# A gated two-layer block on one Trainium2 core: routing from unscaled rows, late work between expert steps, zeroing in two parts, GpSimd's clears between batches

## What is computed

```python
x = x + tanh(g_xattn[0]) * _L0_xattn_ref(ctx_512, _layernorm(x), ...)
x = x + tanh(g_ffn[0]) * _L0_ffn_ref(_layernorm(x), gate_w, w13, w2)
x = x + tanh(g_xattn[1]) * _L1_xattn_ref(_layernorm(x), ctx_512, ...)
x = x + tanh(g_ffn[1]) * _L1_ffn_ref(_layernorm(x), ...)

# _L0_xattn_ref: sim = Q K^T; each row keeps its 76 largest entries, sigmoid, made symmetric
# _L0_ffn_ref, NUM_EXPERTS = 64, TOP_K = 8:
logits = x @ gate_w.T
probs = softmax(logits); topk_w, topk_idx = top_k(probs, 8)
for e in range(64):
    h = silu(x @ w13_e[:128].T) * (x @ w13_e[128:].T)
    out += combine[:, e] * (h @ w2_e.T)
```

## Time and profile before

| | us |
|---|---|
| median of 3 runs | 563.62 |
| lowest and highest | 560.38, 567.36 |
| profiled execution, own time | 561.23 |
| its span in the profile | 559.3 |
| last scatter of a batch's rows starts | 137.56 |
| first matmul of the expert steps | 142.85 |

### The profile page before, as it was taken

One profiled execution on the slowest core, in us unless ns is written; L12 is line 12 of the kernel. 1 busy time (PEld: TensorE's weight loads), 2 busy tenths in 40 slices (PEclk: granted clock), 3 DMA queues, 4 the chain that ended last, 5 costly groups with the idle time before them and its releaser, 6 DMA issues.

```text
span 559.3 us, 9235 instructions
## 1 busy us (share of the span) xinstructions
PE 412.9 (74%) x2738; PEld 347.8 (62%) x2738; DVE 344.4 (62%) x1053; ACT 184.5 (33%) x377; POOL 148.6 (27%) x156
## 2 busy tenths in 40 slices
PE   5345642500799999999823676799789988998796
PEld 3234441400798888988622554797678867996695
DVE  4988876279334444443346893488667885680664
ACT  3122220100233333343236143524453354427321
POOL 4017775757000000000477723330424000000000
PEclk9999999755699999999965879799999999999999
DMA  7999222237599999999832201110212000000000
GB/s 238 424 416 403 91 94 76 94 112 282 146 293 303 324 317 313 331 355 385 279 98 75 86 22 56 39 39 2 59 39 75 2 0 0 20 1 2 2 19 20
DMA packets 36789, 82.96 MB, mean 148 GB/s; under 512 B 6032, under 2 KB 16144, under 8 KB 34960
## 3 DMA queue, kind: packets, MB, share of 16 engines
q1 hardware_dynamic: 23616, 56.48, 29.2%
q0 software_dynamic: 6144, 16.79, 9.4%
q10 hardware_dynamic: 6992, 9.24, 4.6%
HBM read 50.44 MB, written 31.92 MB: 147 GB/s over the span
## 4 chain that ended last, share of the span: by engine, by line
PE 50%; DVE 13%; issue 12%; POOL 7%; ACT 7%; SPq 4%; DMA 3%; another core or an unknown queue 2%; ACTq 1%; DVEq 0%; POOLq 0%
PE PS L606 9%; POOL slots_in L447 7%; PE PS L616 6%; PE PS L695 5%; PE PS L772 3%; PE PS L708 3%; PE PS L709 3%; PE PS L710 3%; PE PS L593 2%; PE PS L669 2%; DMA XE<-slots_in 2%; PE PS L790 2%; PE PS L800 2%; PE PS L757 2%
## 5 line engine op out<-in xcount | busy, mean ns | idle before, releaser
L454 POOL DMA_INDIRECT GB<-slots_out,IDXG x64 | 70.2, 1096 | 221.1 <-DMA slots_out<-OE 133.3
L606 PE MATMUL PS<-XTE,WR 128*128 128x128 f32 (+2 forms) x512 | 80.5, 301 | 0.0
L447 POOL DMA_INDIRECT slots_in<-XNA,IDX x64 | 64.9, 1014 | 38.3 <-issue 30.8
L606 PEld LDWEIGHTS PS<-XTE,WR 128*128 128x128 f32 x512 | 71.2, 195 | 0.3
L1302 DVE TENSOR_TENSOR HE<-SGE,PS 128x128 f32<-128x128 f32 (+2 forms) x64 | 19.9, 312 | 71.7 <-ACT SGE L927 66.3
L616 PE MATMUL PS<-WR,HE 128*80 128x256 f32 (+2 forms) x198 | 53.3, 380 | 0.5 <-issue 0.5
L918 ACT COPY XTE<-PS 128x256 f32<-128x256 f32 (+2 forms) x64 | 26.3, 410 | 73.1 <-PE PS L593 72.0
L708 PE MATMUL PS<-XH,WGH 128*128 128x256 f32 x160 | 50.3, 314 | 0.0
L593 PE MATMUL PS<-CF,XE 80*128 80x80 f32 (+2 forms) x198 | 28.6, 258 | 26.2 <-DMA XE<-slots_in 26.0
L695 PE MATMUL PS<-WD,XW 128*128 128x256 f32 x160 | 42.6, 389 | 5.8 <-DVE TH L1391 5.8
L593 PEld LDWEIGHTS PS<-CF,XE 80*128 80x128 f32 (+2 forms) x198 | 22.9, 145 | 36.5 <-DMA XE<-slots_in 29.7
(11 more groups left out here) (226 smaller groups left out, 814.9 us busy)
## 6 DMA issues: line engine op xcount, KB each, us to landing
WR<-in_wexp SPq DMA_DIRECT2D x64, 384.0 KB
slots_in<-GB SPq DMA_DIRECT2D x12, 1024.0 KB, 18.5
XE<-slots_in SPq DMA_DIRECT2D x24, 160.0 KB, 4.4
slots_out<-OE ACTq DMA_DIRECT2D x24, 160.0 KB
XE<-slots_in SPq DMA_DIRECT2D x29, 128.0 KB, 4.3
slots_out<-OE ACTq DMA_DIRECT2D x24, 128.0 KB
WGU<-in_wgu SPq DMA_DIRECT2D x1, 2560.0 KB
XE<-slots_in SPq DMA_DIRECT2D x11, 192.0 KB, 4.1
```

What stands on the lines that cost most here:

```text
L447: pool.indirect_dma_start(out=xs, out_offset=bass.IndirectOffsetOnAxis(ap=IDX[:, t, j:j + 1], axis=0), in_=XNA[:, t, :], in_offset=None, b ...
L454: pool.indirect_dma_start(out=GB[:, t % BT, j, :], out_offset=None, in_=ys[0:rows, :], in_offset=bass.IndirectOffsetOnAxis(ap=IDXG[:, t, j ...
L606: last = mm(psGE[place % 2][:, a, 0:cap(place)], W13[:, k, a, :], XTE[:, place % 2, k, 0:cap(place)], start=(k == 0), stop=(k == KC - 1))
```

## The change

Seven edits, in words; the diff below has the core of each.

1. Routing uses X1 itself. TensorE transposes X1, and the logits come from X1 times a gate whose column means over D were taken out (centre_gate: two products into psN, two additions on VectorE). The row's scale no longer changes which 8 are largest; it enters in the exponential (scale=RSN, a bias from the new `bias_ready`). XNA is still written, for the scatters.
2. mix adds both BASE products ahead of the wait for `masked`.
3. ranks uses MSUM, the sum of earlier masks, in place of one product per earlier tile. In the last batch the two counts are formed ahead of the ranks, and `counted` is gone.
4. The top rounds are shared out by FIRST_ROUNDS and LATER_ROUNDS.
5. The zeroing is 8 copies of the lower 128 slots of the experts (`zeroed_low`) and then 4 of the upper 64 (`zeroed`). GpSimd waits for the first before tile 0 and for the second before tile 1. norm_scale stands behind 12 scatters. The clears stand at the start of batches 1, 2 and 3, the copy of CTB with the last.
6. VectorE's work behind ORD is cut into pieces, set between its expert steps at places 1 to 12 and 29 to 34 (35 only ends it).
7. SP loads AHEAD = 3 weights before it waits for the scatters, and 5 behind.

ScalarE's scores and base of b + 2 now stand ahead of the exponential of b. The general path makes its own transposes of XNA.

```diff
+ROOT_BEHIND = 12
+LOW = 128
+AHEAD = 3
+FIRST_ROUNDS = (1, 2, 2, 3)
+LATER_ROUNDS = (3, 4, 4, 5)
...
-            for i in range(SLOTS // (8 * P)):
-                sp.dma_start(xs[i * 8 * P:(i + 1) * 8 * P, :].rearrange("(p r) d -> p (r d)", p=P), ZERO)\
-                  .then_inc(S["zeroed"], 16)
+            by_expert = xs.rearrange("(e c) d -> e c d", c=CAP)
+            for first, rows, signal in ((0, LOW, "zeroed_low"), (LOW, CAP - LOW, "zeroed")):
+                experts = P * 8 // rows
+                for e in range(0, E0, experts):
+                    part = by_expert[e:e + experts, first:first + rows, :].rearrange("e (q r) d -> q e (r d)" if rows > experts else "e (q r) d -> e q (r d)", r=8)
+                    sp.dma_start(part, ZERO).then_inc(S[signal], 16)
...
-            for e in range(RING):
-                load_slots(e, first[e])
+            for e in range(AHEAD):
+                load_slots(e, first[e])
+            for e in range(AHEAD, RING):
+                n = expert(e)
+                load_slots(e, n)
+                load_weights(e, n)
...
+            def set_between(b):
+                if b == 1:
+                    nc.gpsimd.memset(VA[:, :, :, :], 0.0).then_inc(S["pool_set"], 1)
+                    nc.gpsimd.memset(G14[:, :, :], 1.0e30).then_inc(S["pool_set"], 1)
+                    nc.gpsimd.memset(TP[:, :, :], 1.0e30).then_inc(S["pool_set"], 1)
+                elif b == 2:
+                    nc.gpsimd.memset(MOE[:, :, :], 0.0).then_inc(S["pool_set"], 1)
+                elif b == 3:
+                    pool.wait_ge(S["pool_set"], 4)
+                    nc.gpsimd.memset(VA[:, :, :, HD:HD + 1], 1.0).then_inc(S["pool_set"], 1)
+                    nc.gpsimd.tensor_copy(CTB[:, :], CT[:, 0:N]).then_inc(S["e_ctx"], 1)
...
-            pool.wait_ge(S["zeroed"], 16 * (SLOTS // (8 * P)))
+            pool.wait_ge(S["zeroed_low"], 16 * (E0 * LOW // (8 * P)))
             for t in range(TT):
+                if t == 1:
+                    pool.wait_ge(S["zeroed"], 16 * (E0 * (CAP - LOW) // (8 * P)))
+                if t % BT == 0:
+                    set_between(t // BT)
                 pool.wait_ge(S["xn_ready"], t // BT + 1)
                 pool.wait_ge(S["idx_ready"], t // BT + 1)
                 for j in range(TOP0):
-                    if t % BT == BT - 1 and j == POW_AT and t // BT + 1 < B:
-                        norm_scale(t // BT + 1)
+                    b = t // BT + 1
+                    if b < B and t % BT * TOP0 + j == ROOT_BEHIND:
+                        norm_scale(b)
...
+            def centre_gate():
+                pe.wait_ge(S["half_set"], 3)
+                for k in range(KC):
+                    last = mm(psN, MINUS_MEAN[:, :], GATE0[:, k, :], start=(k == 0), stop=(k == KC - 1))
+                last.then_inc(S["gate_summed"], 1)
+
             def logits(b):
-                pe.wait_ge(S["xn_ready"], b + 1)
+                pe.wait_ge(S["x1_kept"], b + 1)
...
-                        last = nc.tensor.transpose(psX[:, k, t * P:(t + 1) * P], XNA[:, b * BT + t, k * P:(k + 1) * P], ident)
+                        last = nc.tensor.transpose(psX[:, k, t * P:(t + 1) * P], X1[:, b * BT + t, k * P:(k + 1) * P], ident)
...
+                if b == B - 1:
+                    parts = [MSUM[:, :]] + own
+                    for i, part in enumerate(parts):
+                        mm(psN, onesb, part, start=(i == 0), stop=(i == BT))
+                    for i, part in enumerate(parts):
+                        mm(psC, part, onesb[:, 0:1], start=(i == 0), stop=(i == BT))
+                for t in range(BT):
+                    earlier = ([MSUM[:, :]] if b else []) + own[0:t]
...
+            def between(place):
+
+                early = (count_rows, set_flag, output_keys, output_rows, token_weights, split_weights)
...
                 if place:
                     copy_out(turn, place - 1)
+                if isinstance(turn, int):
+                    between(place)
```

More of the change, by code:

```diff
@@ L573, in _ @@
                     scores(b + 2)
-            for n in range(TT):
-                last = mm(psN, onesb, MB[:, n, :], start=(n == 0), stop=(n == TT - 1))
-            for n in range(TT):
-                last = mm(psC, MB[:, n, :], onesb[:, 0:1], start=(n == 0), stop=(n == TT - 1))
-            last.then_inc(S["counted"], 1)
             pe.wait_ge(S["order_set"], 1)
@@ L631, in all_tokens @@
             def all_tokens():
+                for b in range(B):
+                    pe.wait_ge(S["xnt_copied"], B + b)
+                    for k in range(KC):
+                        for t in range(BT):
+                            last = nc.tensor.transpose(psX[:, k, t * P:(t + 1) * P], XNA[:, b * BT + t, k * P:(k + 1) * P], ident)
+                    last.then_inc(S["xn_flipped"], 1)
+                pe.wait_ge(S["xnt_copied"], 2 * B)
                 with pe.Fori(0, E0 // 2) as i:
@@ L910, in _ @@
                     base(b + 2)
+                act.wait_ge(S["bias_ready"], b + 1)
+                act.wait_ge(S["rs_ready"], b + 1)
+                for t in range(BT):
+                    n = b * BT + t
+                    last = A.activation(C0[:, n, :], psL[:, t, :], ACT.Exp, scale=RSN[:, n, 0:1], bias=SM[:, n, 0:1], accum_out=SM[:, n, 1:2])
+                last.then_inc(S["exp_done"], 1)
             A.preload_act_table(ACT.Silu)
@@ L945, in all_tokens @@
                         act.wait_ge(gathered[t][j], 16)
+                for b in range(B):
+                    act.wait_ge(S["xn_flipped"], B + b + 1)
+                    A.copy(XNT[:, :, b * N:(b + 1) * N], psX).then_inc(S["xnt_copied"], 1)
                 with act.Fori(0, E0) as e:
@@ L1173, in choose @@
                 st.wait()
-                st.done(V.tensor_scalar(SM[:, b * BT:(b + 1) * BT, 0:1], L8[:, :, 0:1], -1.0, None, ALU.mult))
                 for t in range(BT):
@@ new lines, in output_keys, with output_rows @@
+            def output_keys():
+                st.wait()
+                st.done(V.tensor_scalar(FM[:, 2:3], FM[:, 1:2], SKIP, -1.0, ALU.mult, ALU.add))
+                st.done(V.tensor_tensor(KEY2[:, :, :], KEY[:, :, :], ROW[:, 1:2, :].to_broadcast([P, TT, E0]), ALU.add))
+                st.wait()
+                st.done(V.tensor_tensor(KEY2[:, :, :], KEY2[:, :, :], MB[:, :, :], ALU.mult))
+            def output_rows():
+                st.wait()
+                for t in range(TT):
+                    st.done(V.max(K8[:, t, :], KEY2[:, t, :]))
+                st.wait()
+                st.done(V.tensor_scalar(IDXG[:, :, :], K8[:, :, :], FM[:, 2:3], None, ALU.add))
@@ L1280, in _, with row_matches @@
+            def row_matches(t):
                 st.wait()
```

176 lines of the change are left out of this document (102 added, 74 removed).

## The result

| | before | after |
|---|---|---|
| median of the runs, us | 565.49 (4 runs) | 570.65 (3 runs, 568.94 to 571.42) |
| ratio, with 95% interval | | 1.0107 (1.0063 to 1.0150) |
| profiled execution, own time, us | 561.23 | 568.94 |

The changed kernel is 1.1% slower, by less than the 2% that separates "slower" from "same". I had predicted 555.0 us, 1.5% faster; 570.65 lies outside the range of 549 to 563. The three executions of the kernel after are its fast ones: a fourth took 1034.32 us and is left out as slow.

The account below looks back on a forecast made before the run. The end of GpSimd's scatters in routing was taken as the bound. With the stall they end at 132.0 us, 6.5 earlier than 138.53: 561.2 - 6.5 = 554.7, leaned up to 555 us, range 549 to 563.

Parts of the forecast that it names:

- Part 4: Zeroing: high copies led by 8 use 8 engines, so GpSimd stalls 3.0 to 5.4 us, taken 4.1, before its ninth scatter.
- Part 2: GpSimd's routing queue: clears add up to 3.7 us; without a stall batch 3 starts at 107.6 us, fewer rank products saving 0 to 1.5.
- Part 1: Routing from unscaled rows: the first scatter starts at 38.2 us instead of 43.22.
- Part 3: Last batch's scatters: 1.28 us each, 20.2 us against 22.2; 0.7 comes back if weight loads caused the slow ones.
- Part 5: Expert steps: VectorE's moved pieces cost 0, up to 1 us; three weights ahead cost 0, or 6 us if loads limit.
- A: Zeroing: no stall, high copies run on all engines, scatters end at 127.8 us, total 550.5 us; chance 0.24.
- C: Ninth scatter waits much longer for the high zeroes, with four engines a 22.4 us stall, total 573 us; chance 0.07.
- B: Expert stage eats the early gain through late weight loads (6 us) or VectorE's pieces delaying HE, total 561 us; chance 0.12.
- D: Clears and late ranks starve GpSimd's queue 2 to 3 us more, total 557 us; counted within the main case's 0.57.

Follow-up runs that it names:

- z1: Changed kernel with GpSimd's power (norm_scale) behind 10 scatters instead of 12, high zero copies still led by 8: 559.12 us, ratio 1.0024.
- x3: Kernel before with only the zeroing in two parts (high copies led by 8) and GpSimd's two waits: 566.4 us, ratio 1.0049.
- w1: Kernel before with norm_scale behind 12 scatters of a batch instead of 10: 566.58 us, ratio 1.0179.
- v1: Changed kernel with only the high zero copies led by 16 instead of 8, power behind 12 scatters: 548.43 us, ratio 0.9851.
- z4: Changed kernel with high zero copies led by 16, power behind 10 scatters, eight weights loaded ahead instead of three: 550.61 us, ratio 0.9895.
- w3: Changed kernel with high zero copies led by 16, power behind 10, clears as before the change, eight weights ahead: 548.01 us, ratio 0.9824.
- z2: Changed kernel with high zero copies led by 16, power behind 10 scatters, clears as before the change: 548.64 us, ratio 0.9855.
- Set 4: Four runs sharing one chip, w1, z2 again, w3 and w4, each against the kernel before: ratios 1.0179, 0.9850, 0.9824 and 0.9867.
- w4: Changed kernel with high zero copies led by 16, power behind 12, plus a GpSimd wait for the next batch's logits: 548.2 us, ratio 0.9867.
- x1: Changed kernel with only the high zero copies led by 16, the same kernel as v1 on another chip: 561.7 us, ratio 0.9969.

## Why the prediction was wrong

**The step that failed is Part 4's size of the stall**, "3.0 to 5.4 us of stall, I take 4.1". The mechanism was right, with its place, its 8 engines and its engine count in packets. The measured stall is 11.61 us (9.23 in z1, on another chip). Against the predicted clock of the queue:

| | predicted, us | after, us | late by |
|---|---|---|---|
| first scatter | 38.2 | 37.35 | -0.9 |
| ninth | 52.5 | 59.18 | 6.7 |
| batch 1 starts | 65.0 | 72.11 | 7.1 |
| batch 2 | 88.3 | 99.75 | 11.5 |
| batch 3 | 111.8 | 124.78 | 13.0 |
| last scatter ends | 132.0 | 144.95 | 13.0 |

The missed stall is the first 7 us. Of it, 2 are already there when the low copies end, beside the slower issuing: the eighth was issued at 17.1 us and landed 16.9 us later, at 34.0 instead of 31.8. At 213 GB/s the four high ones would then be done at 34.0 + 19.7 = 53.7; the ninth scatter starts 5.5 us behind that. These lie, as I read it, in the time shared with eight scatters and with what SP had queued behind. I had put half of the scatters' bytes at the copies' rate there, up to 2.4 us, and taken 1.1. x3 points the same way: its scatters begin five us later, and the copies land 3 us earlier. How the sharing goes in detail wasn't tried.

Part 4's two bounds came from a sum of bytes. What I left out, and what the 5.5 us suggest without proving it, is that a copy on half of the engines loses twice: the other half can't help it, and packets of others on its half delay it. The Trainium skill, DMA: Bandwidth & Descriptors, section on why a DMA increments its semaphore by 16 and not by 1, gave the number of engines, and the 32 missing packets agree with it.

**The other 6 us** arise at batches 2 and 3. Batch 2 adds 4.4 us and batch 3 1.5: GpSimd waited 4.57 and 3.32 us for IDX, where the forecast had 0 and 1.3. In front of these waits stand the choice's 5.95 us at batch 2 and KEY's 4.53 at batch 3. This is the second step that failed: Part 2 had no term for a late signal at batch 2, and at batch 3 it put down the 3.25 us from mask to KEY to the ranks' products, "worth 0 to 1.5". The row said "remote" in brackets, and 1.14 us is what KEY waits where signals are prompt (w1, v1). I read a wait without a releaser as work.

From the last scatter on, the profile of after has 1.7 us less up to the last HE and 3.0 us more behind it than the profile before. So 13.0 of the 14.2 us by which that execution missed its forecast (568.94 against 554.7) are there when the scatters end.

**Point by point.** Part 1 held: 37.35 us against 38.2, and 5.9 us earlier than before. Part 2's queue held where nothing disturbed it: v1 starts its batches at 61.55, 85.44 and 107.28 us and ends at 127.43, predicted for no stall 60.9, 84.2, 107.6 and 127.8. What it lacked was a term for the late IDX. Part 3 held: 124.78 to 143.97 us is 15 steps of 1.28, and w1, which has the old order on VectorE, still needs 1.42 (119.59 to 140.86). The doubt that it left, whether the traffic of the eight weight loads made the slow steps, is settled by z4 and w3: they issue all eight beside the last batch (z4 from 107.2 to 116.7 us), and their steps stay at 1.28. Part 5 held: the stage from last scatter to last HE is 137.7 us before, 136.0 in after and v1, 137.2 in w3 with eight weights ahead; there is no loss in it, nor much gain.

**The rivals.** A, no stall, is v1: 550.5 foretold, 548.43 measured, though against a before of 558.6 there (0.981 foretold, 0.985 measured). C, a much longer wait, is what came, at half its size: the ninth scatter at 59.2 us lies on the point that I had named as break-even, 59.1, and with that the late signals behind it decided the sign, as far as one execution shows. I had given C 0.07, because I weighed it only as a copy on four engines; a rival should be weighed at its break-even first. Whether the sign would have been the same on a chip with prompt signals is open. B didn't come. D's clears cost what was counted only where IDX is early: z2 against z4, last 3.3 us earlier, the medians 2 apart with overlapping intervals.

**The clock** isn't it. TensorE was granted 0.52 to 0.56 from 30 us on in the routing of after, where before held 1.00 up to 90 us and had 0.66 from there to 137; but so was v1 (0.56 from 60 to 90 us, 0.54 to 137), the kernel with the earliest scatters of its set.

**Open.** What makes the signals late; and what the kernel after itself measures on a chip without them: it was not run there. Its nearest kin, z1, was no slower than before (1.0024). Set 4 also hints at what the unscaled rows bring: the old routing pays for a power behind 12 scatters (w1, 1.0179, the rows wait 4.82, 3.28 and 4.73 us for it and the logits wait for the rows), while w4, with logits from X1 and the power behind 12 too, is at 0.9867. The two differ in the other edits as well.

## What to carry to other kernels

Before you gate a queue on part of a transfer, count the engines that this part is led by: the same bytes led by 8 instead of 16 cost 6.7 us at the last scatter and 7 to 8.5 in time here, about all that this change is worth. When a wait has no releaser in the profile, don't give its time to the work in front of it; put it down as unknown and widen. And compare two versions only on the same chip in the same set: the same kernel moved by 1.2% against the same reference, and a wait that I had added was "proved" to help by nothing but that.

## What the runs showed of the hardware

The next engine can get TensorE's signals 2 to 6 us later in some runs than in others, for the same instructions: 5.1 us from the start of batch 1's logits to the choice in x1 (55.89 to 61.03), 2.0 in v1 (53.30 to 55.27). Four 1 MB copies to HBM led by 8 moved 217 GB/s while they were nearly alone (34 to 38 us in after), and the same stretch in x1, led by 16, 425. A copy to HBM whose destination skips between experts takes SP 1.45 us to issue, a plain one 0.52, and for twelve of them that comes to 8.6 us before the last is in the queue (22.8 against 14.2). GpSimd's mean scatter pitch in the last batch is 1.42 us in the three traces with VectorE's two-input 128x512 operations beside it (before, x3, w1), with single steps from 1.27 to 1.76, and 1.28 in those of the kernels that have them elsewhere, also beside eight weight loads.
